# Two attention layers of a decoder block as one software pipeline of 16 steps, with queries and keys stacked by DMA

## The chip, the cores and the metric

The kernel runs on one core of one Trainium2 chip. The metric is the device time of one execution in microseconds. A core has TensorE (PE: a 128 x 128 array that multiplies, its weight loads are shown apart as PEld), VectorE (DVE), ScalarE (ACT), GpSimd (POOL) and SyncE (SP), which here only issues DMAs. The engines run their own instruction streams in order and meet at semaphores. Operands lie in SBUF, 128 partitions wide; TensorE writes its results to PSUM, eight banks of 512 fp32 columns per partition.

## The reference

x is 8 sequences of 256 tokens with 128 channels. Three layers follow each other, each with a layernorm ahead and a residual behind: local attention, cross attention, and a quantised feed-forward part that the change barely touches.

```python
x = x + attn(layernorm(x))            # 16 heads of 8 channels
#   chunks of 64 queries, each sees its chunk and the one before it, causal
#   q, k, v = layernorm(x) @ w_qkv;  softmax(q k / sqrt(8)) v;  @ w_out
x = x + xattn(layernorm(x), ctx, mask)  # all 256 queries see all 256 keys
#   q = x Wq.T + bq; k, v = ctx Wk.T + bk, ctx Wv.T + bv; key mask; out @ Wo.T + bo
x = x + ffn(layernorm(x))             # 8-bit activations, ternary weights,
#   up to 512, depthwise convolution of 3 taps, silu, down to 128
```

The result has to keep close to fp32, so queries and keys, which go through the array in bf16, are carried as three bf16 parts (high, mid, low).

## The kernel before, in words

Each attention layer is a block of its own, made by `attention(cross)`; between the blocks all engines meet. A block has one step per sequence, 8 steps. In a step of sequence b the scores and outputs of b are made, the maxima of b+1, and the layernorm and projection of b+2, so the first step of each block is preceded by a prologue that fills this pipeline.

**Stacks.** A head has 8 channels. One query in its three parts and one key in its three parts are laid out as slots of 8 rows, six slots for a head, 48 rows in all, plus a row for the key mask (`MROW`) and a row for the maximum. A score is then one contraction over those rows. Two heads share a 128-row operand, one on rows 0 to 63 and one on rows 64 to 127; `QT[:, p, pr, j, :]` holds head j of pair pr, with zeros on the other half, so a matmul contracts all 128 rows and one key operand serves two heads.

**How they are made.** `x_turn` turns the normalised x by the array, `qk_project` makes q and k with the tokens on the partitions (four matmuls for a sequence, fp32). ACT rounds them to `high` (`high_copy`), DVE makes `rest` and copies `high` into the slots of `q_stack` and `k_stack` (L704), POOL writes the mid and low slots (L841, L845). `stack_turn` then turns the stacks by the array, 32 bf16 transposes a step (L346), and ACT (L600) and DVE (L710, L717) copy them from PSUM into `QT` and `KT`, which are double-buffered.

**Maxima.** The softmax needs the row maximum ahead of the scores, since it enters the contraction as a row. `max_scores` multiplies queries by keys with the queries on the output partitions (L390 in the local layer, 64 columns wide tiles, with the causal mask added by a matmul of its own, L384; L380 in the cross layer), DVE takes the negative maximum (L732), `max_turn` turns it (L402), ACT copies it to `mT` (L628), and SP sends `mT` as two DMAs into the last row of `QT` on both row halves (L888). The next step's scores wait for those.

**Scores.** `scores` makes them with the keys on the partitions (L415 cross; L418 for the mask and L422 local), in pairs of PSUM banks, and ACT takes the exponential of 1024 columns at once (L615). `pv` multiplies by V in tiles of 32 columns (L442 cross, L452 local), then follow the copy (L622), the turn of the output (L467), the division (L739, L741), another turn (L475) and its copy (L633), `project` (L483, L486) and the residual (L747).

**What sets the order.** It is written out by hand, for each engine apart, in the functions called `step`. On TensorE a step is: stack_turn x4, scores, value projection, the o_turns, then the maxima of the next sequence with the rest put between them. On SP there is little else but the rows.

```python
                def rows(b, p):
                    sp.wait_ge(mT_sb, b + 1)
                    for j in range(2):
                        sp.dma_start(QT[64 * j + MROW:64 * j + MROW + 1, p, :, j, :],
                                     mT[j * PAIRS:(j + 1) * PAIRS, :]).then_inc(m_row, 16)
```

## Time and profile before

| | us |
|---|---|
| median of 3 runs | 489.31 (488.92 to 489.31) |
| the profiled execution | 489.09 |
| its span in the trace | 487.3 |
| first local scores begin | 59.76 |
| last local scores begin | 191.98 |
| first cross scores begin | 245.04 |
| last cross scores begin | 397.60 |
| last residual of the attention ends | 414.71 |

The span is what the trace covers; the 1.8 us between it and the execution's own time lie around it. The table cuts the span into a setup, the seven local steps between first and last, the passage from the one layer to the other, the seven cross steps, the last step's end, and the feed-forward part of 72.6 us.

### The profile page before, as it was taken

To read this page: it belongs to the slowest core of one execution; us is meant where nothing else is said; L and a number is where in the kernel's file an instruction comes from. 1 tells how busy PE (TensorE), PEld (TensorE's weight loads), DVE (VectorE), ACT (ScalarE), POOL (GpSimd) and SP (SyncE) were. 2 spreads that over 40 slices of the span, in tenths; PEclk is the share of its full clock that TensorE was granted. 3 is DMA by queue.
4 is the path that set the end of the run, shared out by engine and by line. 5 is a ranking of instruction groups with operands and counts; after the bars stand their busy time and mean duration, and the time that the engine had idled before them with its cause. 6 is when DMAs were issued, how large, how long until landed. Compare 5 with 4: busy or idle time off the path is not lost. (4 is left out here: it accounts for less than half of the span.)

```text
span 487.3 us, 11267 instructions
## 1 busy us (share of the span) xinstructions
PE 373.3 (77%) x4174; PEld 235.1 (48%) x4174; DVE 302.4 (62%) x710; ACT 208.4 (43%) x296; POOL 167.2 (34%) x242
## 2 busy tenths in 40 slices
PE   0155898898898987625887879797888877399995
PEld 0044566676676665424254544445454543144452
DVE  6285655665665753214866768676677731489975
ACT  1012155445455354312156566556565655133332
POOL 8251431522504313044315233241505191534400
PEclk9987599999999999957599999999999989599998
DMA  8300000000000000000000000000000000000000
GB/s 253 113 0 2 1 3 2 4 3 1 1 0 1 0 1 1 3 0 1 0 2 1 2 3 1 1 0 1 1 0 1 0 1 2 1 5 17 17 24 27
DMA packets 7884, 6.02 MB, mean 12 GB/s; under 512 B 816, under 2 KB 6960, under 8 KB 7856
## 3 DMA queue, kind: packets, MB, share of 16 engines
q1 hardware_dynamic: 6896, 4.07, 2.9%
q10 hardware_dynamic: 960, 1.57, 0.9%
q8 instruction: 18, 0.29, 0.3%
q14 instruction: 10, 0.08, 0.1%
HBM read 4.46 MB, written 1.05 MB: 11 GB/s over the span
## 5 line engine op out<-in xcount | busy, mean ns | idle before, releaser
L732 DVE TENSOR_REDUCE negm<-ps 128x2 bf16<-128x512 f32 (+1 forms) x192 | 123.6, 685 | 24.3 <-PE ps L390 17.3
L615 ACT ACTIVATE probs<-ps 128x1024 f32<-128x1024 f32 x96 | 97.9, 1024 | 47.6 <-PE ps L415 28.2
L841 POOL TENSOR_SCALAR q_stack<-rest 128x512 bf16<-128x512 f32 x18 | 27.8, 1545 | 93.0 <-DVE rest L696 93.0
L380 PE MATMUL ps<-KT,QT 128*128 128x256 bf16 x256 | 47.7, 289 | 13.0 <-DVE negm L732 11.9
L600 ACT COPY QT<-ps 64x1024 bf16<-64x1024 bf16 x32 | 32.2, 1005 | 42.7 <-PE ps L346 42.7
L346 PE MATMUL ps<-identb,q_stack 128*128 128x128 bf16 x256 | 22.9, 242 | 34.4 <-ACT o_sb L622 10.8
L969 PE MATMUL ps<-tapw,xqT 128*128 128x512 f32 x96 | 45.0, 606 | 0.0
L710 DVE COPY QT<-ps 64x1024 bf16<-64x1024 bf16 x32 | 22.2, 695 | 36.0 <-PE ps L346 36.0
L380 PEld LDWEIGHTS ps<-KT,QT 128*128 128x128 bf16 x256 | 18.8, 99 | 44.2 <-DVE negm L732 40.2
L415 PE MATMUL ps<-QT,KT 128*128 128x512 bf16 x128 | 38.5, 385 | 2.1 <-DMA QT<-mT 2.1
L836 POOL TENSOR_TENSOR k_stack<-ones,mask_t 128x32 bf16<-128x32 f32 x9 | 4.0, 447 | 100.4 <-DVE rest L696 100.4
L346 PEld LDWEIGHTS ps<-identb,q_stack 128*128 128x128 bf16 x256 | 17.1, 108 | 42.0 <-issue 29.9
L739 DVE RECIPROCAL rden<-ps 128x16 f32<-128x16 f32 x32 | 8.1, 252 | 45.8 <-PE ps L467 45.8
L442 PE MATMUL ps<-probs,V 128*32 128x256 f32 x512 | 34.2, 385 | 0.6 <-ACT probs L615 0.6
L696 DVE TENSOR_TENSOR rest<-ps,high 128x512 f32<-128x512 f32 x18 | 12.4, 691 | 32.6 <-ACT high L593 32.6
L390 PE MATMUL ps<-KT,QT 128*64 128x128 bf16 x512 | 27.4, 231 | 0.0
L384 PE MATMUL ps<-mask_q,identb 128*128 128x512 bf16 x64 | 25.5, 398 | 2.0 <-DVE negm L732 1.7
L841 POOL TENSOR_SCALAR k_stack<-rest 128x512 bf16<-128x512 f32 x18 | 26.9, 1494 | 0.0
L969 PEld LDWEIGHTS ps<-tapw,xqT 128*128 128x128 f32 x96 | 18.8, 196 | 16.6 <-issue 16.1
L418 PE MATMUL ps<-mask_k,identb 128*128 128x512 bf16 x64 | 24.6, 384 | 2.5 <-DMA QT<-mT 2.5
L390 PEld LDWEIGHTS ps<-KT,QT 128*64 128x64 bf16 x512 | 16.7, 112 | 17.3 <-issue 17.3
L820 POOL TENSOR_TENSOR ve<-mv,eps 128x2 f32<-128x2 f32 x18 | 3.9, 219 | 60.9 <-DVE mv L689 60.9
(161 smaller groups left out, 716.8 us busy)
## 6 DMA issues: line engine op xcount, KB each, us to landing
X<-in_x_dram SPq DMA_DIRECT2D x2, 512.0 KB, 7.5
out_dram<-ob SPq DMA_DIRECT2D x16, 64.0 KB, 1.5
cwb<-in_L_ffn_conv_w_dram ACTq DMA_DIRECT2D x1, 768.0 KB, 8.2
w_sb<-in_L_ffn_w_dram ACTq DMA_DIRECT2D x2, 256.0 KB, 5.6
QT<-mT SPq DMA_DIRECT2D x32, 4.0 KB
cbrow<-in_L_ffn_conv_b_dram ACTq DMA_DIRECT2D x1, 256.0 KB, 8.8
wqkv_sb<-in_L_attn_w_qkv_dram SPq DMA_DIRECT2D x1, 192.0 KB, 9.1
wout_sb<-in_L_attn_w_out_dram SPq DMA_DIRECT2D x1, 64.0 KB, 8.3
```

The lines of the kernel that those rows point to most:

```text
L346: last = nc.tensor.transpose(ring(i, BF16)[:, pr * P:(pr + 1) * P], src[:, g:g + 2, :].rearrange("p g c -> p (g c)"), identb[:])
L380: last = nc.tensor.matmul(mb[:, u * S:(u + 1) * S], QT[:, p, pr, j, t * P:(t + 1) * P], KT[:, p, pr, W:W + S], start=True, stop=True)
L384: nc.tensor.matmul(mb, identb[:], mask_q[:, t:t + 1, :].to_broadcast([P, 4, P]), start=True, stop=False, skip_group_check=True)
L390: last = nc.tensor.matmul(mb[W * cc:W * cc + W, u * P:(u + 1) * P], QT[:, p, pr, j, k0:k0 + W], KT[:, p, pr, k0:k0 + P], start=False, stop ...
L415: last = nc.tensor.matmul(o, KT[:, p, g, W + i * P:W + (i + 1) * P], QT[:, p, g, :, :], start=True, stop=True)
L418: nc.tensor.matmul(o, identb[:], mask_k[:, min(g, 1):min(g, 1) + 1, :].to_broadcast([P, 8, W]), start=True, stop=False, skip_group_check=True)
L442: last = nc.tensor.matmul(o[32 * r:32 * r + 32, (i % 2) * S:(i % 2) * S + S], V[:, p, t, h, :], probs[:, h // 2, t * 512 + (h % 2) * S:t * ...
L600: nc.scalar.copy(QT[0:SLOT, p, :, 0, t * P:(t + 1) * P], ring(2 * t, BF16)[0:SLOT].rearrange("p (r s) -> p r s", s=P)).then_inc(qT_even, 1)
L615: nc.scalar.activation(probs[:, g, :], ps[:, k:k + 2, :].rearrange("p a n -> p (a n)"), ACT.Exp, scale=SCALE).then_inc(s_exp, 1)
L732: nc.vector.tensor_reduce(o, src, AX.X, ALU.max, negate=True).then_inc(m_max, 1)
L841: nc.gpsimd.tensor_scalar(slots(stack, *mid), repeated(rest[:, i], mid[2]), 1.0, None, ALU.mult).then_inc(mid_done, 1)
L969: last = nc.tensor.matmul(o, xqT[:, b % 2, t * P + k:t * P + k + P], tapw[:, k, :], start=False, stop=(k == 2), skip_group_check=True)
```

## The change

The two blocks become one, with 16 units: unit u below 8 is the local attention of sequence u, from 8 on the cross attention of sequence u - 8. One loop, written out, runs over all 16, so the cross layer's projections and maxima for its first sequences are made in the last local steps. Normalisation runs six units ahead, the turn five, the projection four. Two units make a group g that is projected at once: `q_project` and `k_project` are one fp32 matmul of 512 columns each, with the weights as the stationary side, so that channels come out on partitions. Thereby no stack has to be turned: ACT makes `high` (and adds the bias), DVE `rest`, POOL `mid` and `low`, all channel on partition, and SP copies them by DMA into the slots of `QT` and `KT`, which are now triple-buffered by group. A DMA takes the 64 partitions of 8 heads and writes 8 partitions; there are 24 for a group (two row halves, six slots, q and k), 64 KB each, and four more for the mask rows of a cross group. `q_stack`, `k_stack`, the 32 transposes, the copies L600, L710, L717 and the masks of 128 x 512 go.

Scores and maxima now contract only the 64-row half on which the head lies: the host gives the heads in an order by which even ones lie on the lower half and odd ones on the upper. A `beat` makes one bank of scores of unit i on one half, and between its matmuls those of one bank of maxima (of unit i+1, or the first of i+2) on the other. A local step has 8 beats, a cross step 16, and the places of everything else are given by beat number in two tables. The exponential is taken of 512 columns at a time. The weights come packed and turned from the host (layout only), so the turns of the weights and of the context go; of the feed-forward weights' quantisation, the steps behind the sums move from DVE to POOL, into steps 3 to 6.

```diff
-                def stack_turn(b, p, i, free):
...
-                    for pr in range(PAIRS):
-                        g = t * H + 2 * pr
-                        last = nc.tensor.transpose(ring(i, BF16)[:, pr * P:(pr + 1) * P],
-                                                   src[:, g:g + 2, :].rearrange("p g c -> p (g c)"), identb[:])
...
+                def q_project(g, o, free):
...
+                    nc.tensor.matmul(o.rearrange("p (e t) -> p e t", e=2), wp[:, WQ_C if is_cross(2 * g) else WQ_L, :],
+                                     xnT[:, g % 3, :, W:W + S], start=True, stop=True).then_inc(qk_ps, 1)
...
+                def beat(i, k):
+
+                    ms = max_range(i, k)
+                    m = ms[0] if len(ms) else None
+                    score_open(i, k)
+                    if m is not None:
+                        max_open(m)
+                    ns = 2 if is_cross(i) else 8
+                    nm = 0 if m is None else 2 if is_cross(max_unit(m)[0]) else 8
+                    for x in range(max(ns, nm)):
+                        if x < ns:
+                            last_s = score_mm(i, k, x)
+                        if x < nm:
+                            last_m = max_mm(m, x)
+                    if not is_cross(i):
+                        last_s = score_mask(i, k)
+                    if nm == 8:
+                        last_m = max_mask(m)
...
+class Local:
+    PV3, OT0, OT1, V, OT, Y, XT, Q, K, PV0, PV1, MT, PV2 = 0, 1, 1, 2, 3, 4, 4, 5, 5, 6, 6, 6, 7
+    A_O1, A_V, A_OT, A_X, A_HQ, A_HK, A_O0, A_M = 1, 3, 3, 4, 5, 6, 7, 7
...
+                def score_open(i, k):
+                    n = before(i) + k
+                    if k == 0:
+                        pe.wait_ge(m_row[i % 2], 32 * (i // 2 + 1))
...
-                def rows(b, p):
-                    sp.wait_ge(mT_sb, b + 1)
...
+                def parts(g, src, n, slots, done):
+                    dst = KT if n else QT
+                    sp.wait_ge(done, 2 * g + n + 1)
+                    for j in range(2):
+                        for slot in slots:
+                            r0 = 64 * j + HD * slot
+                            o = dst[r0:r0 + HD, g % 3, :, :, W:W + S] if n else dst[r0:r0 + HD, g % 3, :, :, :]
+                            sp.dma_start(o, src[64 * j:64 * j + 64, n, :].rearrange("p (e t) -> p e t", e=2)
+                                         ).then_inc(st_in[g % 3], 16)
...
+                def rows(u):
+                    sp.wait_ge(mT_sb, u + 1)
...
+                stacks(0)
+                sp.dma_start(cwb[:].rearrange("p k c -> p (k c)"), taps_in.to_broadcast([P, 3 * FH])).then_inc(f_in, 16)
+                stacks(1)
+                rows(0)
...
+                for i in range(UNITS):
+                    if i + 1 < UNITS:
+                        rows(i + 1)
+                    if i % 2 == 0 and (i + 4) // 2 < GROUPS:
+                        stacks((i + 4) // 2)
```

SP's queue in the local layer before: four rows DMAs, in two pairs, each pair waiting for its copy of the maxima; `l_` marks a semaphore of the local block.

```order
L888 DMA QT<-mT 1x8x256 [waits l_max_copied]
L888 DMA QT<-mT 1x8x256
L888 DMA QT<-mT 1x8x256 [waits l_max_copied]
L888 DMA QT<-mT 1x8x256
L893 UNCONDITIONAL_BRANCH
```

SP's queue from iteration 0 on after: the rows of unit 1, the 24 stack DMAs of group 2, and the rows of unit 2; `high`, `mid` and `low` are both tiles and the semaphores of their being made.

```order
L849 DMA QT<-mT 1x8x256 [waits max_copied]
L849 DMA QT<-mT 1x8x256
L826 DMA QT<-high 8x8x512 [waits high]
L826 DMA QT<-high 8x8x512 x5
L826 DMA KT<-high 8x16x256 [waits high]
L826 DMA KT<-high 8x16x256 x5
...
L826 DMA KT<-low 8x16x256 [waits low]
L826 DMA KT<-low 8x16x256
L849 DMA QT<-mT 1x8x256 [waits max_copied]
```

So the rows of every second unit now stand behind 24 transfers on their queue (28 in a cross group).

TensorE in the middle of a local step before: one group of scores, a multiplication by V, and one bank of maxima; the tile of output partitions by columns is behind the names.

```order
L418 MATMUL ps<-mask_k,identb 128x512 [waits l_probs]
L422 MATMUL ps<-QT,KT 128x128 x4
L418 MATMUL ps<-mask_k,identb 128x512
L422 MATMUL ps<-QT,KT 128x128 x4
L452 MATMUL ps<-probs,V 32x64 [waits l_probs,l_v_copied,l_xT]
L452 MATMUL ps<-probs,V 32x64 x15
L375 REGISTER_ALU
L384 MATMUL ps<-mask_q,identb 128x512 [waits l_maxima]
L390 MATMUL ps<-KT,QT 64x128 x8
```

TensorE at the first beat of local step 0 after: the eight matmuls of a score bank (L290) alternate with the eight of a maxima bank (L254), then come the two masks and the next beat.

```order
L290 MATMUL ps<-QT,KT 128x64 [waits maxima,max_rows0,vector_constants]
L254 MATMUL ps<-KT,QT 64x128
...
L290 MATMUL ps<-QT,KT 128x64
L254 MATMUL ps<-KT,QT 64x128
L296 MATMUL ps<-tri_k,lower 128x512
L260 MATMUL ps<-tri_q,twice 128x4x64
L290 MATMUL ps<-QT,KT 128x64 [waits maxima]
```

Where before eight matmuls of one tile size followed each other, the tile size now changes from each matmul to the next, and with it the row half.

## Rows read from the trace of the kernel before

**Rows 1.** The page: busy time, share of the span and instructions of each engine.

```profile
PE 373.3 (77%) x4174; PEld 235.1 (48%) x4174; DVE 302.4 (62%) x710; ACT 208.4 (43%) x296; POOL 167.2 (34%) x242
```

**Rows 2.** Stretches: length, busy PE, PEld, DVE, ACT, POOL, PE clock, DMA share, GB/s.

```profile
0.00:59.80 59.80, 24.51 (x182) 17.83 (x183) 35.70 (x63) 8.29 (x12) 28.24 (x43) 0.83 0.24 75
59.80:192.00 132.20, 118.15 (x2099) 86.11 (x2098) 79.01 (x157) 64.21 (x89) 42.16 (x52) 1.00 0.01 1
192.00:244.50 52.50, 31.56 (x318) 20.15 (x319) 22.08 (x50) 12.11 (x19) 16.51 (x25) 0.71 0.00 1
244.50:397.60 153.10, 127.56 (x1216) 74.27 (x1215) 107.94 (x213) 92.64 (x124) 51.14 (x70) 1.00 0.00 1
397.60:414.70 17.10, 13.71 (x110) 7.17 (x110) 2.93 (x10) 9.61 (x12) 6.16 (x5) 0.90 0.00 1
414.70:487.30 72.60, 57.78 (x256) 29.61 (x256) 54.74 (x219) 21.51 (x41) 23.04 (x48) 0.90 0.05 15
```

**Rows 3.** Groups in one local step, 103.7 to 123.0: busy, mean ns, idle before.

```profile
L732 DVE TENSOR_REDUCE negm<-ps 128x4 bf16<-128x512 f32 x8 | 5.5, 690 | 1.8 <-PE ps L390 1.8
...
L452 PE MATMUL ps<-probs,V 128*32 128x64 f32 x128 | 2.6, 222 | 0.0
...
L346 PE MATMUL ps<-identb,q_stack 128*128 128x128 bf16 x16 | 1.2, 219 | 1.6 <-ACT o_sb L622 0.9 <-ACT QT L600 0.7
...
L622 ACT COPY o_sb<-ps 128x512 f32<-128x512 f32 x2 | 1.2, 585 | 1.1 <-PE ps L452 1.1
...
L467 PE MATMUL ps<-identf,o_sb 128*128 128x128 f32 x8 | 1.0, 273 | 0.0
```

**Rows 4.** The timeline of TensorE in a local step: start, length, operation.

```profile
109.12 0.38 PE L418 MATMUL ps<-mask_k,identb 128*128 128x512 bf16 x1
...
109.34 0.39 PE L422 MATMUL ps<-QT,KT 128*128 128x128 bf16 x4
...
109.56 0.38 PE L384 MATMUL ps<-mask_q,identb 128*128 128x512 bf16 x1
...
109.87 0.41 PE L390 MATMUL ps<-KT,QT 128*64 128x128 bf16 x8
...
110.22 0.39 PE L384 MATMUL ps<-mask_q,identb 128*128 128x512 bf16 x1
```

**Rows 5.** The timeline ahead of the last local scores: maxima copied, then sent.

```profile
189.09 0.36 ACT L628 COPY mT<-ps 16x256 bf16<-16x256 bf16 x1 [1.42 <-PE ps L402]
189.48 1.32 SPq L888 DMA_DIRECT2D QT<-mT  x2
...
191.98 0.39 PE L418 MATMUL ps<-mask_k,identb 128*128 128x512 bf16 x1 [2.50 <-DMA QT<-mT]
```

**Rows 6.** The timeline of SP's queue in the setup: one load of 64 KB.

```profile
3.51 0.43 SPq L136 DMA_DIRECT2D wraw<-in_L_xattn_Wq_dram  x1
```

**Rows 7.** The stretch in which one rows DMA moves; columns as in rows 2.

```profile
113.86:113.96 0.10, 0.10 (x5) 0.10 (x3) 0.00 (x0) 0.00 (x0) 0.10 (x1) 1.00 0.21 41
```

**Rows 8.** The page, DMA issues: KB each, us from issue to landing.

```profile
X<-in_x_dram SPq DMA_DIRECT2D x2, 512.0 KB, 7.5
```

**Rows 9.** The timeline of the setup: first statistics and first rounded queries and keys.

```profile
21.27 0.49 DVE L686 BATCH_NORM_STATS2 bnst<-X 128x6 f32<-128x128 f32 x2 [0.61 <-PEq L126]
...
27.79 0.58 ACT L593 CAST high<-ps 128x512 bf16<-128x512 f32 x1 [2.17 <-PE ps L329]
```

**Rows 10.** The page's group of fp32 matmuls of 512 columns, two passes each.

```profile
L969 PE MATMUL ps<-tapw,xqT 128*128 128x512 f32 x96 | 45.0, 606 | 0.0
```

**Rows 11.** Groups of the cross layer, 270 to 384: the maxima.

```profile
L732 DVE TENSOR_REDUCE negm<-ps 128x2 bf16<-128x512 f32 x85 | 52.8, 681 | 3.6 <-PE ps L380 3.1
```

**Rows 12.** The timeline from the last exponential to the last residual.

```profile
407.04 1.94 ACT L615 ACTIVATE probs<-ps 128x1024 f32<-128x1024 f32 x2
...
414.29 0.42 DVE L747 TENSOR_TENSOR X<-ps,X 128x256 f32<-128x256 f32 x1 [1.72 <-PE ps L486]
```

1410 lines of the change are left out of this document (673 added, 737 removed).

## The prediction

> **What bounds the kernel now.** The page comes first: TensorE is busy 77% of the span and no other engine more than 62% [rows 1]. That is an average, so the span is cut at the first and last scores of each layer [rows 2]. In the seven steady local steps (132.2 us, 18.9 each) TensorE is busy 89% at full clock: it is the bound, and its instructions are what a step costs. In the seven steady cross steps (153.1 us, 21.9 each) it is busy 83% and VectorE 71%. The setup (59.8 us, PE 41%), the passage between the layers (52.5 us for what takes a step in the steady state, PE 60%) and the last cross step (17.1) are chains of waits; there the PE clock is at 0.71 to 0.90 of full. The feed-forward part takes 72.6 and is left as it is.
>
> Two more rows show what the new order will meet. Between the copy of the maxima to `mT` and the scores that need them lie 2.9 us (189.09 to 191.98): copy 0.36, two DMA issues 1.32, the landing [rows 5]. And in a local step a group of one tile size follows the other at its streaming time: a 512-column mask to the next group of the same size takes 0.22 us; but L422 to the mask L384 0.22, and from that mask to L390, whose tile is 64 wide instead of 128, 0.31 [rows 4]. The change of tile size costs 0.09 us there.
>
> **What goes.** The 32 transposes of a step are 2.4 us of TensorE (two tiles of 1.2) with 1.6 us of waits for their PSUM banks [rows 3]. The masks shrink, the scores contract 64 rows, and the projection of q and k becomes two matmuls of two passes for two sequences. A pass of 512 columns in fp32 keeps the array for 45.0/96 = 0.47 us [rows 10], so four passes for two steps are 0.9 us a step, against 1.1 now. The weights' turns go from the setup. The passage goes wholly: it took 52.5 us against a step of 19, so 33 us, and this gain depends on nothing below.
>
> **The local step, by TensorE.** A beat has eight score matmuls of 64 columns and eight maxima matmuls of 128, then masks of 512 and 256 columns. If the tiles of both row halves flow side by side, that takes the eight of 128 columns (L390: 0.35 from its start to the next mask, 109.87 to 110.22), the longer mask (0.22) and two changes of size (0.1 each), about 0.8 us [rows 4]. The same two banks take 1.10 before: scores 0.44 (mask and four matmuls, 0.22 each), maxima 0.66 (109.56 to 110.22). Eight beats save 2.4 us. So the step is 18.9 less 4.0 for the transposes and their waits, less 2.4, less 0.2 for q and k: 12.3. I add 1.2, for the changes of tile size around four pv, 0.1 going in and 0.1 coming out, and for `max_turn`, which waits for the last maximum on DVE: **13.5**, of which 6.4 are beats and 7.1 the rest. The copy of the maxima stands at the last beat (`A_M` = 7), so the 2.9 us of rows 5 lie bare behind each local step: **16.4** from scores to scores. DVE has eight maxima of 0.69 [rows 3] and 3 us more, 8.5; ACT eight exponentials of 0.59 (L622 has their size [rows 3]) and 2.8 of copies, 7.5; POOL, which had 42.16 in seven steps [rows 2], writes smaller tiles now and has the weights' quantisation besides, which would show only beyond 10 us in a step. All three hide behind TensorE, and would bound a step only if it fell below 9.
>
> **The cross step.** VectorE has sixteen maxima of 0.68 [rows 11], 10.9, and of its 15.4 a step [rows 2] the 4.5 that are not maxima shrink by the copies into stacks and out of PSUM that go (two such copies, each of a maximum's size, are 1.4, the least that goes): 3.1 left, **14.0**. The copy of the maxima stands at beat 13 of 16, so two beats cover 1.6 of the 2.9. **15.5** with it, against 21.9. TensorE has 18.2 busy a step now [rows 2]; without 2.4 of transposes and with two maxima matmuls beside two of the scores in each beat it lies at 12 to 15, below.
>
> **The queue of SP.** This is the term that decides. The change adds 24 DMAs a pair of steps, 28 in cross pairs, on the queue that carries the rows. `rows(i+1)` goes first, then the stacks of a group, and `rows(i+2)` behind all of them. Waiting behind SP's stacks are thus the rows, and behind these the scores of the next step, hence all of TensorE: in every second step the time from scores to scores is not 16.4 but as long as the 24 transfers, plus 1.0 for the rows' own. What one of the 24 costs, D, no row shows. From below: an issue takes 0.43 us for a 64 KB load [rows 6], or 0.66 for a rows DMA (1.32 for two [rows 5]), the nearest in shape, since it writes SBUF from SBUF; I take 0.68 with the gap. From above: the transfer itself, 64 KB into 8 partitions. The nearest row is the DMA that writes into one partition, which moves 41 GB/s [rows 7]: 64 KB at 41 GB/s are 1.6 us. I take D = 1.2, between the two, since 8 partitions should take more than one does, but far from the 128 partitions of a load. Then the late scores come 24 x 1.2 + 1.0 = 29.8 us after the ones ahead, in a cross group, whose four mask rows cost 0.68 each, 32.5.
>
> The Trainium skill bears on this number. "SBUF — State Buffer", section "Door 1", says that the rate of a DMA depends on how many of SBUF's ports its partitions reach; eight neighbouring partitions reach two, at about 27 GB/s each, and by that figure 64 KB would take an estimated 1.2 us. No row here shows a transfer of this shape.
>
> **The sum of the forecast case.** Setup: X lands at about 8.5 (issue at 0.7, 7.5 to land [rows 8]); from first statistics to the rounded q and k of one sequence 7.1 us [rows 9], for a pair, and in two roundings, some 10: 19. The first stacks take 24 x 1.2 to 48, the second to 78, and the rows, behind both, 3 more with the gap: first scores at **81.5** (59.8 before). Local: four pairs, two with the stacks of a local group behind them, 16.4 + 29.8 = 46.2, two with a cross group 16.4 + 32.5 = 48.9: **190.2**. Cross: two pairs with stacks 15.5 + 32.5 = 48: **96.0**. The last four steps have none: 15.5, 15.5, 13.5 (fewer maxima), 11 to the last exponential, and then the 5.7 us that the end took before (408.98 to 414.71 [rows 12]): **61.2**. Feed-forward **72.6** [rows 2]. Together 501.5, and the 1.8 that lie around the span (489.09 against 487.3; the median, 489.31, is 0.2 above that run): **503 us**. Each 0.1 us of D moves it by 19.2 (192 transfers lie on the path: 48 in the setup, 144 in six pairs), so it equals the time before at D = 1.13, and reads 475 at 1.05 and 550 at 1.45. A stall of 14 us a pair also lets the PE clock fall, as it is at 0.71 in the passage [rows 2]; some 1 us a stall, inside the range of D.
>
> **Rivals.**
> *A, the transfers hide behind their issue* (D = 0.68), and the tiles flow side by side. For it: 16 engines share a transfer and 41 GB/s may be the rate of so small a piece, not of the partition. First scores at 56; pairs 16.4 + 17.4 = 34 and 36.8, 141.6 for the local layer; cross pairs 36, 72; then the same 61.2, 72.6 and 1.8: **405**.
> *B, the change of tile drains the array.* The scores' tile is 64 x 128, the local maxima's 64 x 64, and they alternate: 16 changes a beat. Every change in the trace costs, the mask to L390 0.09 us over the stream [rows 4]; with the 0.05 that a small matmul streams each of the 16 becomes 0.15, a beat 2.6 with its masks (0.2), and a local step 20.8 + 7.1 + 2.9 = 30.8. Against it: there the tiles lie on the same rows, here on separate halves. In the cross layer both tiles are 64 x 128 and nothing drains. With D = 0.68, the three pairs with local maxima take 61.6, the fourth 45: 229.8 instead of 141.6, **493**: slower than before, and that as soon as one small matmul with its change takes over 0.146 us.
> *C, both*: pairs of 61.6, 61.6, 63.3 and 57.5, 244 in place of 190.2: **557**.
>
> The Trainium skill, "TensorEngine Tiling (Array Packing)", section "Key Properties", says that changing the tiling mode, not just the tile, drains TensorE; by it B's mechanism holds in the local beats. The trace agrees as far as it goes (0.09 us [rows 4]), but shows no tile of 64 rows.
>
> **How the numbers follow.** Forecast 0.31, A 0.29, B 0.18, C 0.15, other 0.07 (a transfer slower than 1.6, a serial chain I missed, or a faster setup). The forecast case alone spans 475 to 550. The whole range holds A with 15 us below it for shorter beats, and C with little above it: 390 to 560. Within 0.2%, about what a measurement of this kernel can tell, lies little: 0.04. Faster: A whole, 0.09 of the forecast (D under 1.13), 0.07 of B, 0.02 other: 0.47. Slower: 0.49.
>
> **What would show it.** In the profile of the changed kernel: first scores at 81 (D = 1.2) or 56; the scores L290 of every second step with an idle time of some 14 us behind the DMA from `mT`, or about 3; a local beat of 0.8 us or of 2.6, and PE busy in the local layer accordingly; SP's queue never idle from `high` to the rows. The first cross scores right behind the last local ones without a passage: if there is one, the 33 us are wrong. If the first scores come at 56 and a beat is 0.8 us long, A holds and I am wrong by 100 us.

## The result: 681 us, and where the time went

The changed kernel takes 681.25 us (median of 4 runs, 677.44 to 685.41) against 489.12 (4 runs). The ratio is 1.393, with a 95% interval of 1.384 to 1.402. Forecast were 503 us and a range of 390 to 560: the sign was right, the size far off. The prediction gave slower a chance of 0.49 and faster one of 0.47, so the right sign is no more than luck.

The page of the changed kernel, busy time by engine, with the slices of TensorE's clock (tenths of full speed) under it, against rows 1:

```profile
PE 502.1 (74%) x3890; PEld 272.7 (40%) x3890; DVE 233.2 (35%) x587; ACT 176.8 (26%) x346; POOL 116.6 (17%) x184
...
PEclk9755556555565555555555555797896899558999
```

Fewer instructions than before (3890 on TensorE instead of 4174), and 129 us more of busy time on it. The second line says why that is possible: from the setup to past the middle of the span the granted clock stands near half, 1.2 instead of 2.4 GHz. Before it was at full speed in the steady steps [rows 2].

The same span cut at the first exponential of unit 0, of unit 8 (first cross unit) and of unit 12, and at the last residual; columns as in rows 2:

```profile
0.00:77.50 77.50, 25.99 (x149) 12.83 (x149) 23.52 (x56) 6.33 (x12) 22.96 (x53) 0.68 0.59 95
77.50:423.50 346.00, 298.10 (x2287) 171.80 (x2287) 70.76 (x151) 60.45 (x118) 59.56 (x67) 0.51 0.17 19
423.50:521.70 98.20, 59.04 (x633) 29.28 (x629) 50.78 (x97) 45.82 (x92) 11.09 (x16) 0.85 0.27 34
521.70:602.00 80.30, 60.52 (x574) 28.95 (x570) 33.04 (x66) 42.66 (x84) 0.00 (x0) 0.80 0.01 2
602.00:675.60 73.60, 58.44 (x256) 29.82 (x256) 55.15 (x219) 21.51 (x41) 23.02 (x48) 0.89 0.05 15
```

| part | forecast | measured | difference |
|---|---|---|---|
| to the first exponential (the forecast: first scores, measured 73.65) | 81.5 | 77.5 | -4 |
| local layer, eight steps | 190.2 | 346.0 | +156 |
| cross, units 8 to 12 | 96.0 | 98.2 | +2 |
| cross, unit 12 to the last residual | 61.2 | 80.3 | +19 |
| feed-forward | 72.6 | 73.6 | +1 |
| around the span | 1.8 | 1.8 | 0 |

The profiled run took 677.44 us, the median lies 3.8 above it. Nearly the whole miss is the local layer. Its steps, read at the first exponential of each unit, take 42.2, 45.5, 50.8, 45.6, 52.1, 45.5, 36.4 and 27.9 us. The last two, whose maxima belong in part or wholly to cross units, are the short ones. TensorE is busy 86% of this stretch, so waits are not what fills it.

The timeline of TensorE within a local step, in a beat at half clock, up to the next work behind it:

```profile
139.99 0.23 PE L290 MATMUL ps<-QT,KT 50*128 50x64 bf16 x1
140.15 0.31 PE L254 MATMUL ps<-KT,QT 49*64 49x128 bf16 x1
140.39 0.23 PE L290 MATMUL ps<-QT,KT 50*128 50x64 bf16 x1
...
142.43 0.61 PE L296 MATMUL ps<-tri_k,lower 64*128 64x512 bf16 x1
142.43 0.39 PE L260 MATMUL ps<-tri_q,twice 64*128 64x256 bf16 x1
142.96 1.22 PE L384 MATMUL ps<-wp,oT 128*128 128x128 f32 x4
```

A score matmul (L290) and a maxima matmul (L254) start one behind the other and take 0.40 us a pair, though they lie on different row halves and different banks. The two masks, which have one tile size, start together at 142.43 and do run side by side. In one of the few stretches at full clock the pair takes 0.30 us:

```profile
102.95 0.20 PE L290 MATMUL ps<-QT,KT 50*128 50x64 bf16 x1
103.08 0.24 PE L254 MATMUL ps<-KT,QT 49*64 49x128 bf16 x1
103.26 0.20 PE L290 MATMUL ps<-QT,KT 50*128 50x64 bf16 x1
```

In the cross beats, where both have the tile 64 x 128, they start within 0.01 us of each other:

```profile
441.25 0.28 PE L287 MATMUL ps<-QT,KT 50*128 50x256 bf16 x1
441.25 0.28 PE L250 MATMUL ps<-KT,QT 49*128 49x256 bf16 x1
441.37 0.27 PE L287 MATMUL ps<-QT,KT 50*128 50x256 bf16 x1
```

Two theories for the local layer follow. "Drains" means here that a matmul starts only when those before it have left the array. The first: the change of tile size drains the array at each of 16 places a beat, whatever rows the tiles use, and the half clock comes on top of it, from the drains or from something else. The rival: the two row halves in turn, or their few rows, are what costs.

### The profile page after: what moved, and what is told of

Same layout as the page of the kernel before. It is cut to its first block and busy times, and to the rows that moved or that the text cites. A ratio compares the mean times of both kernels' runs of the same rounds, so it can differ in the third digit from the quotient of the medians.

```text
span 675.6 us, 9996 instructions
## 1 busy us (share of the span) xinstructions
PE 502.1 (74%) x3890; PEld 272.7 (40%) x3890; DVE 233.2 (35%) x587; ACT 176.8 (26%) x346; POOL 116.6 (17%) x184
## 5 line engine op out<-in xcount | busy, mean ns | idle before, releaser
L609 DVE TENSOR_REDUCE negm<-ps 128x2 bf16<-128x512 f32 (+1 forms) x192 | 129.0, 688 | 354.7 <-PE ps L260 264.0
L505 ACT ACTIVATE probs<-ps 128x512 f32<-128x512 f32 x192 | 112.0, 598 | 372.4 <-PE ps L296 283.5
L254 PE MATMUL ps<-KT,QT 49*64 49x128 bf16 x512 | 134.2, 309 | 16.6 <-DMA KT<-low 14.0
L290 PE MATMUL ps<-QT,KT 50*128 50x64 bf16 x512 | 104.5, 232 | 20.8 <-issue 15.2
L290 PEld LDWEIGHTS ps<-QT,KT 50*128 50x128 bf16 x512 | 48.7, 106 | 82.2 <-issue 33.4
L254 PEld LDWEIGHTS ps<-KT,QT 49*64 49x64 bf16 x512 | 55.2, 129 | 48.9 <-issue 20.2
L287 PE MATMUL ps<-QT,KT 50*128 50x256 bf16 x256 | 46.9, 302 | 29.9 <-DMA QT<-mT 27.3
L250 PE MATMUL ps<-KT,QT 49*128 49x256 bf16 x256 | 52.7, 310 | 0.0
L343 PE MATMUL ps<-probs,V 128*32 128x256 f32 x512 | 39.4, 432 | 11.3 <-ACT o_sb L511 9.6
L352 PE MATMUL ps<-probs,V 128*32 128x64 f32 x1024 | 32.1, 309 | 17.2 <-ACT o_sb L511 11.2
L287 PEld LDWEIGHTS ps<-QT,KT 50*128 50x128 bf16 x256 | 16.8, 98 | 57.5 <-DMA QT<-mT 29.5
L296 PE MATMUL ps<-tri_k,lower 64*128 64x512 bf16 x64 | 38.2, 597 | 0.0
L352 PEld LDWEIGHTS ps<-probs,V 128*32 128x32 f32 x1024 | 26.3, 166 | 27.7 <-ACT o_sb L511 15.3
L910 PEld LDWEIGHTS ps<-tapw,xqT 128*128 128x128 f32 x96 | 19.1, 199 | 16.9 <-issue 16.4
L343 PEld LDWEIGHTS ps<-probs,V 128*32 128x32 f32 x512 | 14.4, 118 | 27.1 <-ACT o_sb L511 12.1
L260 PE MATMUL ps<-tri_q,twice 64*128 64x256 bf16 x64 | 24.9, 388 | 0.0
```

Of the source, the lines that this page charges most:

```text
L250: return nc.tensor.matmul(o[:, x * S:(x + 1) * S], QT[r, s, pr, e, t * P:(t + 1) * P], KT[r, s, pr, e, W:W + S], start=True, stop=True)
L254: return nc.tensor.matmul(o[W * cc:W * cc + W, x // 2 * P:(x // 2 + 1) * P], QT[r, s, pr, e, k0:k0 + W], KT[r, s, pr, e, k0:k0 + P], start ...
L260: return nc.tensor.matmul(o.rearrange("p (r s) -> p r s", s=P)[:, :, W:P], twice[64 * j:64 * j + 64, :], tri_q[64 * j:64 * j + 64, :].unsq ...
L287: return nc.tensor.matmul(o[:, x * S:(x + 1) * S], KT[r, s, pr, e, W + kt * P:W + (kt + 1) * P], QT[r, s, pr, e, :], start=True, stop=True)
L290: return nc.tensor.matmul(o[:, x * W:(x + 1) * W], KT[r, s, x, e, W * c:W * c + P], QT[r, s, x, e, W * c:W * c + W], start=(x == 0), stop= ...
L296: return nc.tensor.matmul(bank(n % 3).rearrange("p (r q) -> p r q", q=W), lower[64 * j:64 * j + 64, :], tri_k[64 * j:64 * j + 64, :].unsqu ...
```

## The experiments

The kernels below were run once each, `h1_wide_max` and `h2_cross_pairs` four times. The four runs of the changed kernel span 8 us, so differences of a few us between single runs say little.

### The two kinds of matmul apart, and with one tile size

`e1_apart`, in `beat`:

```diff
+                    apart = not is_cross(i)
                     for x in range(max(ns, nm)):
                         if x < ns:
                             last_s = score_mm(i, k, x)
-                        if x < nm:
+                        if x < nm and not apart:
                             last_m = max_mm(m, x)
                     if not is_cross(i):
                         last_s = score_mask(i, k)
+                    if apart:
+                        for x in range(nm):
+                            last_m = max_mm(m, x)
```

> The changed kernel, with the eight score matmuls of a local beat and their mask first and the eight maxima matmuls behind them, instead of one by one in turn; the cross beats are left as they are. It leaves nothing out. Theory 1, the change of tile size (64 x 128 and 64 x 64) drains the array, and the half clock comes of that: 2 changes a beat in place of 16, a local beat of 1.2 to 1.4 us instead of 3.7, the granted clock back at 1.0 in the local steps, a step of 20 to 24 us instead of 47, the whole 470 to 510 us. Rival 2, the half clock comes of tiles that use 49 or 50 rows, in whatever order: clock 0.5 still, a beat of 2.3, a step of 34 to 38, the whole 580 to 610.

`e2_same_tile`, in `max_mm`:

```diff
-                    k0 = W * (2 * t + cc)
-                    return nc.tensor.matmul(o[W * cc:W * cc + W, x // 2 * P:(x // 2 + 1) * P], QT[r, s, pr, e, k0:k0 + W],
-                                            KT[r, s, pr, e, k0:k0 + P], start=(x < 2), stop=False, skip_group_check=True)
+                    return nc.tensor.matmul(o[:, x * W:(x + 1) * W], QT[r, s, pr, e, t * P:(t + 1) * P],
+                                            KT[r, s, pr, e, W + t * P + cc * W:W + t * P + (cc + 1) * W],
+                                            start=(x == 0), stop=False, skip_group_check=True)
```

> The changed kernel, in which a local maxima matmul takes 128 queries and 64 keys instead of 64 queries and 128 keys, so that its tile is 64 x 128 as that of the scores; their number and the turn by turn order stay. The maximum is then one over the 128 keys of the query's own half of the sequence, which is another number to take off before the exponential and not another softmax. Theory 1, only the change of tile size drains: both row halves flow side by side, a beat of 0.8 to 1.0 us at full clock, a local step of 16 to 20, the whole 430 to 470 us. Rival 2, few rows mean half clock: a beat of 1.4 to 1.8, a step of 28 to 32, the whole 530 to 570. Rival 3, the turn from one row half to the other stalls by itself: as the changed kernel, 660 to 690.

Measured: 573.1 us for `e1_apart` and 533.1 for `e2_same_tile`. The local layer of the two, as in the table above (first exponential of unit 0 to that of unit 8):

```profile
74.80:313.30 238.50, 200.12 (x2297) 125.06 (x2296) 69.97 (x151) 61.02 (x119) 59.64 (x67) 0.53 0.24 28
```

```profile
74.00:271.00 197.00, 132.70 (x2284) 89.29 (x2278) 69.83 (x152) 60.06 (x119) 59.59 (x67) 0.66 0.28 34
```

And the timeline of a beat in `e2_same_tile`, at full clock, up to its masks:

```profile
184.74 0.20 PE L290 MATMUL ps<-QT,KT 50*128 50x64 bf16 x1
184.74 0.20 PE L253 MATMUL ps<-KT,QT 49*128 49x64 bf16 x1
184.78 0.19 PE L290 MATMUL ps<-QT,KT 50*128 50x64 bf16 x1
...
184.98 0.38 PE L296 MATMUL ps<-tri_k,lower 64*128 64x512 bf16 x1
```

With one tile size the eight pairs take 0.24 us instead of 2.4, turn by turn and from one row half to the other as before; these maxima matmuls stream 64 columns instead of 128, which explains at most an estimated 8 x 0.03 of it. So the turn between row halves costs nothing measurable, and the beat's time was the change of tile size. `e1_apart` changes only the order, stays at half clock (0.53), and its layer is 107.5 us shorter; with one tile size 149 us go, about as much as the whole miss of 156, some of it by a clock of 0.66 instead of 0.51. Neither expectation came out whole, though. 573.1 lies in neither range. 533.1 lies in that of the rival, few rows (530 to 570), but with a beat far below its 1.4 us and a local step of 24.6 us on average, which neither had. And the clock did not come back with the drains gone.

The Trainium skill has the rule for the drain in "TensorEngine Tiling (Array Packing)", section "Key Properties": changing the mode, not just the tile, drains the engine. The traces agree with both halves of it: 0.30 us a pair with two sizes (changed kernel), 0.03 with one size on two tiles (`e2_same_tile`).

### The kernel before with 48 changes of tile a step

`f1_before_mixed` makes three of the eight maxima banks of a local step turn by turn with scores:

```diff
+                    for x in range(8):
...
+                        last_s = nc.tensor.matmul(o[:, x % 4 * 2 * W:(x % 4 + 1) * 2 * W],
+                                                  KT[:, p, x, W * g:W * g + P], QT[:, p, x, :, W * g:W * g + W],
+                                                  start=False, stop=(x % 4 == 3), skip_group_check=True)
...
+                        last_m = nc.tensor.matmul(mb[W * cc:W * cc + W, u * P:(u + 1) * P],
+                                                  QT[:, q, pr0 + u, j, k0:k0 + W], KT[:, q, pr0 + u, k0:k0 + P],
+                                                  start=False, stop=(u == 3), skip_group_check=True)
```

> The kernel before, in whose local layer three of the eight banks of maxima of a step are made turn by turn with the scores (eight score matmuls, tile 128 x 128, and eight of maxima, tile 128 x 64), so 48 changes of tile size a step more, with all else as before. Theory 1, drains whatever the rows: such a pair takes 0.30 us at full clock, as in the changed kernel, and 24 of them 7.2 in place of 3 x 0.8, so the local step grows from 19 to 23 to 25 us at clock 1.0 and the whole by 30 to 45 us; if drains of that share also bring the clock down, to over 30 a step and by over 90. Rival, drains only with tiles on separate row halves: within 10 us of before.

Measured: 529.4 us, 41.6 over the kernel before on the same chip (487.8), and a local step of 24.9 instead of 19.2. Its timeline, and its local layer up to the first exponential of unit 7:

```profile
95.80 0.24 PE L428 MATMUL ps<-KT,QT 128*64 128x128 bf16 x1
95.97 0.23 PE L424 MATMUL ps<-QT,KT 128*128 128x128 bf16 x1
96.13 0.24 PE L428 MATMUL ps<-KT,QT 128*64 128x128 bf16 x1
```

```profile
61.90:233.30 171.40, 155.32 (x2097) 103.70 (x2097) 78.43 (x155) 63.85 (x89) 42.20 (x52) 1.00 0.00 1
```

A pair takes 0.33 us on tiles of all 128 rows too, so the drain needs no separate row halves. The step and the whole lie in the ranges of the first theory. And the clock stays at 1.00: drains in three of eight banks do not bring it down.

### What holds the clock down

Few active rows were the rival. Five runs bear on it. `g1_half_rows` is the kernel before with the maxima on 64 rows, and `g2_half_rows_all` puts its scores on 64 rows too, a bank per row half:

```diff
-                                    QT[:, p, pr, j, k0:k0 + W],
-                                    KT[:, p, pr, k0:k0 + P],
+                                    QT[64 * j:64 * j + 64, p, pr, j, k0:k0 + W],
+                                    KT[64 * j:64 * j + 64, p, pr, k0:k0 + P],
```

> The kernel before, whose maxima matmuls in both layers contract only the 64 rows on which their head lies (slices 64j to 64j+64 of QT and KT; the rows left out hold zeros), nothing moved, the same columns. If few active rows alone bring the granted clock down, it falls to 0.5 to 0.7 in the local steps, where these matmuls are a third of the stream, and the whole rises by 40 us or more. If the clock falls only where TensorE starts little in a given time (waits, drains), it stays at 1.0 and the time within 5 us of before.

> As g1_half_rows (the kernel before, maxima on 64 rows), with the scores on 64 rows too: a bank takes the heads of one row half, in matmuls of half the columns, so the columns of the stream stay and no tile size changes more often than before. g1_half_rows left the local clock at 1.00 and the cross clock at 0.97 (488.6 to 496.1 us). If active rows decide, with now two thirds of a step's columns on half of them the local clock falls to 0.5 to 0.7, a local step to 25 to 35 us and the whole to over 560. If what decides is how much TensorE idles, the clock stays over 0.95 and the whole at 490 to 505.

`e7_all_rows` goes the other way, the changed kernel on all rows, with its drains; each score is then the sum of two heads, so it leaves out the separation of heads and is no attention:

```diff
-                r = slice(64 * j, 64 * j + ROWS + 1)
+                r = slice(0, P)
...
-                    r = slice(64 * j, 64 * j + ROWS + 2)
+                    r = slice(0, P)
```

> The changed kernel, in which all matmuls of scores, maxima and their masks contract all 128 rows (tiles 128 x 128 and 128 x 64, turn by turn as in it) instead of one row half; the two tiles are set to zero once in the setup, which lengthens it by some 12 us. Every score is then the sum over two heads, so what it computes is not attention, and the exponential is taken with a small scale; the number of instructions and columns is that of the changed kernel. Theory 1, the drains bring the clock down: it stays at 0.5 in the local layer, a step at 42 to 48 us. Theory 2, the clock is at 0.5 because few rows of the array are active in nearly all of the stream: clock 0.9 to 1.0, with the drains 0.30 us a pair, a local step of 30 to 36 us, which is what the prediction's case B had; in the cross layer the two halves no longer run side by side.

Measured: 496.1 and 514.0 us for the two on the kernel before (488.6 and 489.0 on their chips), with the local clock at 1.00 and 0.99 and the cross clock at 0.97 and 0.92; and 687.2 for `e7_all_rows`, whose local layer takes 343.0 us at a clock of 0.57. In g1 and g2 the local clock stayed up, against the theory of few rows, but the whole lies above what the other one gave too (7.5 us more than before for at most 5, and 514 us for at most 505). `e7_all_rows` came out as the drain theory had it (42 to 48 us a step at half clock). So few rows do not halve the clock of a stream that also has full rows, and full rows do not give it back to one drained at every matmul.

So the next question was whether TensorE streams too little. Three kernels make every score mask of a local beat three times, a dense stream of 3.4 us more a step at full clock:

```diff
                     if not is_cross(i):
-                        last_s = score_mask(i, k)
+                        for _ in range(3):
+                            last_s = score_mask(i, k)
```

> As e1_apart (573.1 us, local clock 0.53), with the score mask of every local beat added three times instead of once: 16 matmuls of 512 columns more in a local step, 3.4 us of TensorE at full clock and 6.8 at half; masked scores become -3e30, the softmax is the same. If TensorE is at half clock since it streams too little between waits, the local clock rises above 0.7 and the whole stays within 15 us of e1_apart or falls below it. If the tiles themselves hold the clock down: clock 0.5, 8 x 6.8 us more, the whole 620 to 630.

> As e2_same_tile (533.1 us, local clock 0.66), with the score mask three times in every local beat, as in k1_apart_dense. If too little streams: clock over 0.85 in the local layer, and since part of the 24 us of a step is waiting that the masks fill, the whole 515 to 540. If the tiles hold the clock down: clock at 0.66 or below, the step 4 to 6 us longer, the whole 565 to 580.

> The changed kernel (681.3 us, local clock 0.51) with the score mask three times in every local beat. Here TensorE waits little for others: a beat of 3.7 us is 3.3 us of changes of tile, in which the array is drained. If a drained array counts as one that streams too little, the added 0.4 us of stream a beat may lift the clock in part (0.6 to 0.8), and the whole is 640 to 700; if it lifts it fully, a pair costs 0.30 instead of 0.41 and the whole falls to 620. If the clock stays at 0.51, the masks cost 6.8 us a step: 730 to 740.

Measured: 629.1, 571.2 and 731.9 us; the local clock 0.52, 0.65 and 0.53. Eight steps of 3.4 us would be 27 us at full clock and 54 at half. 56, 38 and 51 us came over the kernels without the added stream, so it was paid at about the clock that each kernel had. Streaming more, on 64 rows, did not lift the clock.

The last two put rows and stream together. `k4_full_row_masks` is `k1_apart_dense` with the three masks on 128 rows (same columns), and `k5_apart_all_rows` is `e7_all_rows` with scores and maxima apart, full rows without drains:

```diff
-                    return nc.tensor.matmul(bank(n % 3).rearrange("p (r q) -> p r q", q=W), lower[64 * j:64 * j + 64, :],
-                                            tri_k[64 * j:64 * j + 64, :].unsqueeze(1).to_broadcast([64, 8, W]),
+                    return nc.tensor.matmul(bank(n % 3).rearrange("p (r q) -> p r q", q=W), lower[:],
+                                            tri_k[:].unsqueeze(1).to_broadcast([P, 8, W]),
```

> As k1_apart_dense (629.1 us, local clock 0.52), with the three score masks of a local beat contracted over 128 rows instead of 64, the same columns and the same softmax; a tile size more changes in a beat. If the clock follows how much of the array works, rows counted, it rises above 0.65 in the local layer and the whole falls to 560 to 600. If rows do not count, the clock stays at 0.52 and the whole rises by the added changes of tile, 5 to 10 us: 630 to 640.

> As e7_all_rows (687.2 us, local clock 0.58; all matmuls of the beats on 128 rows, which computes sums over two heads and not attention), with scores and maxima of a local beat apart as in e1_apart, so that nothing drains but twice a beat. If rows and streaming time together decide, this has the local clock near 1.0, a local step at 18 to 22 us against 28 to 33 in e1_apart, the whole 490 to 530. If the clock stays under 0.6, neither does, and the whole is 580 to 600, 12 us of longer setup included.

Measured: 596.8 and 532.9 us. The local layers of `k1_apart_dense`, `k4_full_row_masks` and `k5_apart_all_rows`, one after the other:

```profile
75.40:365.40 290.00, 253.12 (x2423) 138.32 (x2421) 70.14 (x152) 61.03 (x119) 59.55 (x67) 0.52 0.18 23
```

```profile
75.50:333.60 258.10, 214.44 (x2421) 116.89 (x2421) 70.13 (x151) 60.69 (x118) 59.66 (x67) 0.71 0.22 26
```

```profile
89.30:284.10 194.80, 126.35 (x2294) 87.11 (x2295) 69.19 (x151) 59.86 (x118) 59.72 (x67) 0.88 0.28 35
```

`k5_apart_all_rows`, like e7, is no attention, and its setup is longer by the zeroing of two tiles. With the same columns, and a change of tile size more in each beat, masks on 128 rows instead of 64 raise the clock from 0.52 to 0.71 and take 32 us off. Scores and maxima on all rows, apart, run at 0.88 where those of `e1_apart` run at 0.53, and the layer is 44 us shorter. Put together: the clock stayed up where the stream was dense on few rows beside full-row work (g1, g2), and where it was drained in part on full rows (f1). It stood near half where little of the array worked for long: half of its rows at a time (e1, k1), or full rows with a drain at every matmul (e7), or both, as in the changed kernel. With both halves at once (e2, e5, k2) it lay between, at 0.58 to 0.66. How busy TensorE is does not give this order: 65% of the layer in k5 at 0.88, 91% in f1 at 1.00, but 87% in k1 at 0.52. The runs show this order and no more, each by one run. Why it is so is not shown, and where the limit lies they do not tell.

### The stack transfers

Three kernels build on `e2_same_tile`. `e3_rows_act` has ScalarE issue the rows DMAs, `e6_two_queues` has it issue half of the first two groups' stack transfers, and `e8_high_only` sends 12 of 24 transfers from group 3 on, leaving the mid and low parts of an older group in place:

```diff
                     nc.scalar.copy(mT[:, u % 2, :], src[0:H, 0:S]).then_inc(mT_sb, 1)
+                    act.wait_ge(mT_sb, u + 1)
+                    for j in range(2):
+                        act.dma_start(QT[64 * j + MAX_ROW:64 * j + MAX_ROW + 1, u // 2 % 3, :, u % 2, :],
```

> As e2_same_tile, with the two DMAs of a step's maxima rows issued by ScalarE behind its copy, not by SyncE behind the 24 or 28 stack DMAs. If the rows' place behind the stacks holds up every second step once the local step is short, as the prediction had it with 1.0 to 1.2 us for each transfer, this takes 8 to 12 us off each of six pairs: 50 to 70 us under e2_same_tile. If the stacks hide in the steps, or the rows wait for the same 16 engines whatever their queue, it is within 10 us of it.

> As e2_same_tile, with the upper row half's 12 stack DMAs of each of the first two groups issued by ScalarE on its own queue, at the same time as the lower half's by SyncE; from group 2 on as before. If a transfer is bound by the 8 partitions that it writes (64 KB in 1.0 us, 64 GB/s, in e2_same_tile), two queues write 16 partitions at once: the rate in the setup doubles to over 100 GB/s, the first scores come 15 to 20 us earlier, the whole 515. If the 16 engines or the queue's packets bound it, the rate stays at 62 to 70 GB/s and the time within 5 us of e2_same_tile.

```diff
                     for part, (src, done) in enumerate(((high, high_done), (mid, mid_done), (low, low_done))):
+                        if g >= 3 and part:
+                            continue
```

> As e2_same_tile, with only the high parts of queries and keys sent from group 3 on: 12 transfers a group instead of 24 (16 instead of 28 in a cross group). The mid and low slots then keep those of an older group, so scores are off by rounding parts. If the 24 transfers hold the steps (64 KB in 1.0 us each, rows behind them), the cross pairs at units 8 to 12, now 49.8 and 54.5 us, fall to 36 to 40, the local pairs behind group 3 by up to 10, the whole to 490 to 500. If the local step of 24 us is a chain of hand-overs, its pairs stay at 48 to 50 and only the cross pairs fall: 505 to 515. If the transfers are hidden, nothing moves: 530.

Measured: 544.8, 535.3 and 500.3 us, against 533.1. The second came out as one of its cases had it, the third nearly so, the first in neither of its cases. First the size of a transfer. In the changed kernel SP issues the 24 of group 2 from 114.7 to 131.1 us, 0.66 each and a little between. Two stretches of that time and one behind the last issue, the last column in GB/s:

```profile
118.00:124.00 6.00, 6.00 (x58) 3.41 (x58) 0.69 (x1) 0.60 (x1) 0.00 (x0) 0.50 0.61 66
...
130.00:136.00 6.00, 4.69 (x22) 3.03 (x21) 1.60 (x5) 0.60 (x1) 0.00 (x0) 0.50 0.63 73
136.00:139.00 3.00, 3.00 (x15) 1.50 (x14) 0.30 (x1) 0.34 (x1) 0.00 (x0) 0.50 0.48 62
```

The queue moves some 65 GB/s, 64 KB in 1.0 us, and goes on for 8 us behind the last issue. The prediction had D = 1.2, between an issue of 0.68 and 1.6; the measured D is 1.0. In `e6_two_queues`, with two queues writing both row halves at once, the rate at the same place is 72 instead of 68 GB/s:

```profile
49.00:55.00 6.00, 4.93 (x58) 3.67 (x59) 5.94 (x15) 0.00 (x0) 4.66 (x9) 0.50 0.61 72
```

So the 8 partitions written are not what limits it, since 16 at once are hardly faster. The estimate of 1.2 us that the prediction works out from the Trainium skill's port rates ("SBUF — State Buffer", section "Door 1") lies near the measured 1.0, but this run speaks against the ports as the reason here. What does limit the rate stays open. The rows gain nothing from a queue of their own (e3): they wait less before their scores, 22 us instead of 53 in all for L290 and L287, but ScalarE's own stream, which now holds two DMA issues and a wait, keeps the pv matmuls (L352, L343) waiting for `o_sb` 44 us instead of 21. This hides what the queue alone is worth: even its steps without transfers (units 12 to 15) take 24.1, 23.5 and 21.2 us instead of 21.4, 16.7 and 16.8.

What the transfers cost is shown by `e8_high_only`. Its two cross pairs, units 8 to 10 and 10 to 12, take 41.4 and 37.1 us instead of 49.8 and 54.5 (46.7 to 54.5 in the other kernels on the changed one), and the stretch of both is:

```profile
264.00:342.50 78.50, 58.12 (x633) 28.51 (x629) 50.57 (x96) 45.86 (x91) 11.15 (x16) 0.92 0.18 22
```

TensorE's waits for the rows in the cross units 8 to 12, in the changed kernel (423.5 to 521.7) and in `e8_high_only` (264.0 to 342.5), as us in total, times, longest:

```profile
PE ps L287 <- DMA QT<-mT: 21.7, 4, 12.3
```

```profile
PE ps L287 <- DMA QT<-mT: 3.1, 4, 1.2
```

Its local pairs behind unit 2 (45.6, 51.2, 52.1 against 50.4, 48.3, 57.5) move by 3 to 5 us, one of them up, no more than single runs of like kernels differ by. The 28 transfers thus bind the cross steps, as the prediction had it, and are hidden in the local ones by whatever makes those 24 us long.

### What makes a local step 24 us long without drains

`e5_fewer_max` is `e2_same_tile` with four maxima matmuls of 128 columns a bank and no mask behind them:

```diff
-                    t, pr, cc = k // 4, 4 * (k // 2 % 2) + x // 2, x % 2
-                    return nc.tensor.matmul(o[:, x * W:(x + 1) * W], QT[r, s, pr, e, t * P:(t + 1) * P],
+                    t, pr = k // 4, 4 * (k // 2 % 2) + x
+                    return nc.tensor.matmul(o[:, x * P:(x + 1) * P], QT[r, s, pr, e, t * P:(t + 1) * P],
```

> As e2_same_tile, with four maxima matmuls of 128 columns in a local beat instead of eight of 64, and no mask behind them: TensorE has less to do in every local beat, and nothing else changes. If the local step of e2_same_tile (24 us) is a chain of hand-overs between TensorE, ScalarE and VectorE, in which the beats only fill gaps, the step stays at 23 to 25 and the whole at 525 to 535. If TensorE's own work bounds it, a beat of 0.35 loses some 0.05 to 0.1 and more at half clock, 8 x 0.1 a step: 515 to 525.

Measured: 539.8 us, 7 more than with more work, and above both expectations. Its local layer takes 207.0 us at clock 0.58, against 197.0 at 0.66. TensorE's waits in `e2_same_tile` from unit 1 to unit 7 (six steps: us in total, times, longest):

```profile
PE ps L352 <- ACT o_sb L511: 8.4, 6, 1.4
PE ps L232 <- DVE o_tok L619: 8.4, 6, 1.9
PE ps L366 <- ACT o_sb L511: 6.8, 6, 1.2
...
PE ps L205 <- DVE X L626: 2.9, 3, 1.2
```

Smaller ones come on top, and 9.9 us in four times for the rows. Without the rows, TensorE stands 5.5 us of each step at hand-overs to ScalarE and VectorE, 1.1 to 1.4 at each of the three that come in every step. My reading is that the short beat between two places no longer covers the way to another engine and back. The rest of the 24 us is its own work, two thirds of the layer at half clock (a mean of 0.66). Less work in the beats of `e5_fewer_max` bought nothing. Whether it lowers the clock is not sure: the kernels whose local beats are those of `e2_same_tile` (e2, e8, e6, e3) spread over 0.66, 0.64, 0.62 and 0.61 by themselves, and the layer of `e6_two_queues` is 5.7 us longer than that of e2. How much of the 24 us each of the two takes was not separated.

### Is a part of the change worth having

`h1_wide_max` is the kernel before with the idea of `e5_fewer_max`, maxima in the tile of the scores:

```diff
-                        nc.tensor.matmul(mb, identb[:], mask_q[:, t:t + 1, :].to_broadcast([P, 4, P]),
-                                         start=True, stop=False, skip_group_check=True)
...
+                            last = nc.tensor.matmul(mb[:, u * P:(u + 1) * P], QT[:, p, pr, j, t * P:(t + 1) * P],
+                                                    KT[:, p, pr, W + t * P:W + (t + 1) * P], start=True, stop=True)
```

> The kernel before, with the local maxima taken over 128 queries by the 128 keys of their own half of the sequence: four matmuls of 128 columns in a 128 x 128 tile for a bank, in place of a mask and eight in 128 x 64. What is taken off before the exponential is then another number, at most 10.1 under and 19 over the true maximum on these inputs; the softmax is the same. A bank costs 0.22 us instead of 0.66 and has no change of tile size; eight banks save 3.5 us of a TensorE step of 17.4. If TensorE still bounds the step, eight steps save 24 to 28 us: 461 to 465. If the chain of hand-overs through the two shared PSUM banks or the maxima on VectorE bound it next, at 17 to 18 a step: 472 to 480.

Measured: 477.9 us, ratio 0.977 with an interval of 0.971 to 0.983: faster than both kernels, though the interval does not settle whether by 2%. The local step falls from 19.2 to 17.6. A bank of maxima now takes 0.23 us from its start to the next work (100.71 to 100.94), as expected, instead of 0.66:

```profile
100.71 0.40 PE L386 MATMUL ps<-KT,QT 128*128 128x128 bf16 x4
100.94 0.38 PE L411 MATMUL ps<-mask_k,identb 128*128 128x512 bf16 x1
```

That is 3.4 us less for TensorE a step, of which 1.6 arrive; it is busy 82% of the layer now instead of 89. The maximum taken off is over other keys than the softmax's, so with inputs far larger than these the exponential could overflow, which the kernel before excludes.

`h2_cross_pairs` is `h1_wide_max` with all cross scores and maxima on tiles of 64 x 128, and with the cross beats of the change, side by side on two row halves, for five of eight score groups:

```diff
+                    for h in range(2):
+                        pe.wait_ge(m_max, NM * (b + 1) + i + h - 1)
+                        for x in range(2):
+                            last_s = score_mm(b, p, g, 1 - h, x)
+                            last_m = max_mm(b + 1, 1 - p, i + h, x)
```

> As h1_wide_max (477.9 us), with one piece of the change taken over into the cross layer: scores and maxima of the cross layer on 64 x 128 tiles, and in five of the eight score groups of a step the score matmuls alternate with those of a maxima bank on the other row half, same tile size, so that two banks are made in the time of one. Nothing else moves but five places of the hand-written order. The changed kernel has such a cross step at 16.6 us where no stack transfers are under way, against 22.2 before. If TensorE's own time bounds the cross step, ten banks of 0.22 us are hidden, 2.2 us a step, 14 to 18 us in all: 460 to 464. If the 32 transposes and their copies, or the chain of hand-overs, bound it, the cross step stays at 21 to 22.2: 472 to 478. Should half of the array at work bring the clock below 0.95, as in g2_half_rows_all (0.89), over 480.

Measured: 510.9 us, ratio 1.048 (1.041 to 1.054). Against `h1_wide_max` that is 33 us more. The cross step is 26.9 us instead of 22.2. The group of its score matmuls over six cross steps (busy, mean ns, idle before):

```profile
L375 PE MATMUL ps<-QT,KT 64*128 64x256 bf16 x192 | 31.2, 298 | 26.0 <-DVE negm L760 24.6 <-ACT probs L643 0.9
```

Scores never waited for a free maxima bank before; made in turn with maxima they do, 4 us a step, and the clock of the stretch is 0.88. The five places taken over cost more than they hide. The changed kernel has three banks for maxima, this one two; that this is the reason was not tested, and the waits and the clock were not separated.

## Why the prediction was wrong

**What bounds before, the passage, the ends.** Right. The passage is gone: unit 7 to unit 8 is a step of 27.9 us in place of 52.6. The feed-forward part kept its time.

**The queue of SP, called the term that decides.** Its mechanism holds: first scores after an idle time of 14.0 us behind the second group's transfers, waits of up to 12.3 us for the rows in the cross units 8 to 12, and 16.8 to 23.9 us a step there when half of the transfers go, against 22.6 to 28.5. That this stretch came out at 98.2 us for a forecast of 96.0 is partly luck: forecast were steps of 15.5 and 32.5 in turn, measured are 21.9, 24.7, 22.9 and 28.6. D was 1.0 instead of 1.2. It does not decide, since in the local layer the steps are so long that 25 us of transfers hide in two of them.

**The local step, by TensorE.** This is the step that failed: the overlap of the two row halves, and the clock. The step was put at 13.5 us, with tiles of both row halves side by side and a beat of 0.8 us. The beat is 3.4 to 3.8 us and the step, from unit to unit, 43 instead of 24 on average. The prediction had the cause as its case B, with 0.15 us for each small matmul and a beat of 2.6 at full clock. The measured pair of 0.30 says just that. Two things were missed. Case B and its combination with the transfers, case C, had 0.33 together against 0.60 for the cases without drains, though the one row that bore on it, 0.09 us from mask to L390 [rows 4], spoke for drains, and no row for the opposite. And the clock was taken as full but for about 1 us a stall; this term was mis-sized, in case C too, which has the drains and put the local layer at 244 us, 102 under the measured 346. The clock stands at half in nearly all of it (a mean of 0.51), by which the pair takes 0.40 to 0.41, 6.7 us more in a step of 64 pairs, and what is no beat takes some 17 us instead of 10. No row of the kernel before showed the half clock under steady work, only around waits, and the prediction took it to come with waits alone.

**Hand-overs.** With one tile size the layer takes 197.0 us for the forecast's 190.2, but not by its terms: steps of about 24 us instead of 16.4 and 30 in turn. That the total comes near is luck. The 5.5 us a step at hand-overs were not in the sum, but for what `max_turn` waits.

**The cross step.** Where no transfers are under way it is 16.6 us at full clock (units 13 to 15), for a forecast of 15.5. The stretch from unit 12 to the last residual took 19 us more than forecast. Nearly half of that is the last step, 20 us for 11, at a mean clock of 0.57.

**The rivals and the range.** A was out by the drains, B had the beat and C the two mechanisms. All three had one clock, so the range ended at 560, 120 us short.

## What to carry to other kernels

Matmuls of different tile sizes did not overlap here, even on separate rows and banks; before two streams are interleaved on row halves, give them one tile size. A kernel most of whose matmuls use half the rows one at a time, or drain at every matmul, should be costed at half clock as well as at full: no run here gave such a kernel its full clock. When the pieces between two hand-overs get shorter than the way to another engine and back, count the hand-overs: they were 5.5 us of a step of 24 here.

## What the runs showed of the hardware

- A small matmul with a change of tile size ahead of it takes 0.15 us at full clock (0.30 a pair) and 0.20 at half, with tiles on separate row halves (changed kernel) as on the same rows (0.33 with 128-column scores, f1).
- Two tiles of 64 x 128 on separate halves start within 0.01 us of each other and run at once.
- The granted clock of the local layer, by kernel: 1.00 before, f1 and g1; 0.99 g2; 0.88 k5; 0.71 k4; 0.66 e2; 0.65 k2; 0.64 e8; 0.62 e6; 0.61 e3; 0.58 e5; 0.57 e7; 0.53 e1 and k3; 0.52 k1; 0.51 the changed kernel. From k1 to k4 only the rows of a mask changed, and with them one more change of tile size a beat.
- A DMA of 64 KB from 64 partitions to 8 takes 1.0 us in a row of its like (65 GB/s, and 72 with two queues against 68 at the same place), and is issued in 0.66.
